# Order of the splits before the fourth step, and of products and adds at both ends of L1 to L3, in a hand-ordered four-layer kernel

## Reference

```python
# L0: gated MLP with a low-rank adapter per block of 32 rows (rank 16, 16 adapters), F = 1376
t = einsum('bri,bni->bnr', A[idx], x);  gate = x @ W_gate.T + 0.5 * B_gate[idx] @ t   # up alike
act = silu(gate) * up
x = x + (act @ W_down.T + 0.5 * B_down[idx] @ (A_down[idx] @ act))
# L1: each block of 32 rows is mixed by the 32 x 32 matrix of its condition
x = x + einsum('bct,bcd->bdt', x, W1[cond])
# L2: base product plus 8 experts of rank 16; the gates are a softmax over the top 2 logits
logits = x @ Wr.T + 5 * one_hot(lang);  topw, topi = top_k(logits, 2)
gates = sum(one_hot(topi) * softmax(topw))
x = x + x @ W2.T + 2.0 * ((x @ A.T) * gates) @ B
# L3: as L1 with other matrices
x = x + einsum('bct,bcd->bdt', x, W3[cond])
```

## Time and profile before

| | before |
|---|---|
| median of 3 runs | 589.03 us (588.71 to 590.17) |
| profiled execution, its own time | 589.99 us |
| its span, first to last instruction | 588.0 us |
| PE busy | 570.5 us |
| DVE busy | 303.8 us |
| ACT busy | 204.5 us |
| POOL busy | 222.1 us |
| granted PE clock, mean | 0.994 |

### The profile page before, as it was taken

The page is one execution under the profiler, slowest core; times in us unless marked ns, Lnnn a source line. Parts: engine busy times, 40 slices in busy tenths (PEclk is TensorE's granted clock), DMA queues, the critical chain, the costliest instruction groups (busy, mean ns, idle before and its releaser), DMA issues.

```text
span 588.0 us, 8799 instructions
## 1 busy us (share of the span) xinstructions
PE 570.5 (97%) x3371; PEld 514.8 (88%) x3371; DVE 303.8 (52%) x697; ACT 204.5 (35%) x413; POOL 222.1 (38%) x227
## 2 busy tenths in 40 slices
PE   5979999999999999999999999999999999999996
PEld 5768998888898989898998989898989898999995
DVE  4885443434344435343434343444444656878776
ACT  4764233233333333332323323232332523333321
POOL 5432133556565656541313131313130212443431
PEclk9979999999999999999999999999999999999999
DMA  8983324253525353543333242424242821233322
GB/s 273 364 284 103 107 79 133 85 173 98 181 92 182 105 175 113 169 135 102 119 93 127 86 134 78 130 82 135 76 136 72 317 62 54 72 137 134 109 89 72
DMA packets 34890, 77.38 MB, mean 132 GB/s; under 512 B 5217, under 2 KB 9633, under 8 KB 34849
## 3 DMA queue, kind: packets, MB, share of 16 engines
q0 software_dynamic: 10752, 37.23, 19.9%
q1 hardware_dynamic: 23952, 39.56, 19.9%
q10 hardware_dynamic: 144, 0.03, 0.0%
HBM read 64.22 MB, written 12.58 MB: 131 GB/s over the span
## 4 chain that ended last, share of the span: by engine, by line
PE 91%; DVE 4%; DMA 2%; issue 1%; ACT 1%; POOL 1%; POOLq 0%; DVEq 0%; ACTq 0%
PE gu_ps L1148 13%; PE gu_ps L1150 13%; PE gu_ps L1149 13%; PE down_ps L1148 8%; PE down_ps L1149 8%; PE down_ps L1150 8%; PE l_ps L1148 5%; PE l_ps L1150 5%; PE l_ps L1149 5%; PE gu_ps L1155 3%; PE gu_ps L1156 3%; PE act_t L1218 3%; PE x2t_ps L1272 1%; DVE w_sb L928 1%; DMA a_raw<-a_all,idx_batch 1%
## 5 line engine op out<-in xcount | busy, mean ns | idle before, releaser
L666 POOL DMA_INDIRECT b_sel_raw<-b_gu,idx_rank x48 | 47.9, 997 | 195.5 <-PE gu_ps L1156 183.2
L1148 PE MATMUL down_ps<-wd_sb,act_hl 128*128 128x288 f32 (+1 forms) x352 | 105.9, 301 | 0.0
L1148 PE MATMUL gu_ps<-w_sb,xt 128*128 128x512 f32 x256 | 104.7, 409 | 0.0
L1149 PE MATMUL down_ps<-wd_sb,act_hl 128*128 128x288 f32 (+1 forms) x352 | 104.6, 297 | 0.0
L1150 PE MATMUL down_ps<-wd_sb,act_hl 128*128 128x288 f32 (+1 forms) x352 | 104.4, 297 | 0.0
L1150 PE MATMUL gu_ps<-w_sb,xt 128*128 128x512 f32 x256 | 100.6, 393 | 0.0
L1149 PE MATMUL gu_ps<-w_sb,xt 128*128 128x512 f32 x256 | 100.2, 391 | 0.0
L666 POOL DMA_INDIRECT a_raw<-a_all,idx_batch x64 | 74.7, 1167 | 57.7 <-DVE wd_sb L928 38.1
L782 ACT CAST act_hl<-act_t 128x256 fp32r<-128x256 f32 (+1 forms) x64 | 27.3, 453 | 136.5 <-PE act_t L1218 136.4
L773 ACT ACTIVATE act<-gu_ps 128x512 f32<-128x512 f32 (+1 forms) x47 | 26.1, 556 | 130.3 <-PE gu_ps L1156 130.3
L928 DVE TENSOR_TENSOR act_hl<-act_t,act_hl 128x256 fp32r<-128x256 f32 (+1 forms) x64 | 32.0, 521 | 75.2 <-ACT act_hl L782 75.1
(11 more groups left out here) (147 smaller groups left out, 1111.9 us busy)
## 6 DMA issues: line engine op xcount, KB each, us to landing
w_sb_raw<-wgu SPq DMA_DIRECT2D x16, 256.0 KB, 9.7
x_res<-x_rows SPq DMA_DIRECT2D x16, 256.0 KB, 2.9
x_after_l<-x_res SPq DMA_DIRECT2D x16, 256.0 KB, 2.3
bd<-bd_hl SPq DMA_DIRECT2D x16, 256.0 KB, 2.0
x<-x_after_l SPq DMA_DIRECT2D x16, 256.0 KB, 2.7
bd_hl<-bd SPq DMA_DIRECT2D x16, 256.0 KB, 4.2
xt_raw<-x_t SPq DMA_DIRECT2D x15, 256.0 KB, 2.5
out<-y SPq DMA_DIRECT2D x15, 256.0 KB, 2.0
```

Of the source, the lines that this page charges most:

```text
L666: nc.gpsimd.indirect_dma_start(out=dst, out_offset=None, in_=table, in_offset=bass.IndirectOffsetOnAxis(ap=idx, axis=0)).then_inc(s, 16)
L1148: pe.matmul(out_, stationary[0], moving[0], start=start, stop=False, skip_group_check=True)
L1149: pe.matmul(out_, stationary[0], moving[1], start=False, stop=False, skip_group_check=True)
```

## The change

Four edits. (1) In the list for step 2 job ("b", 3) stands right behind ("b", 2), and ("act", 0) and ("gate", 2) change places; on PE gate(3) is no longer cut in two by transpose_t(1), which now comes behind transpose_act(0), and gate(4) comes before down(0). (2) At the seam from L0 to L1 to L3, PE does down_adapters(15) before l1(2), and DVE the residual add of tile 15 before add_x2(2). (3) For tiles 1 and 14 DVE does add_x3 before route_weights instead of between route_weights and route_gates. (4) For the last two tiles PE's and DVE's orders are written out. What is computed, and the number of instructions on each engine, stay the same.

```diff
@@ lane_jobs
-                2: [("b", 2), ("adt", 1)] + wd_items(0) + [("act", 0), ("b", 3), ("gate", 2)],
+                2: [("b", 2), ("b", 3), ("adt", 1)] + wd_items(0) + [("gate", 2), ("act", 0)],
@@ block.vector
+                    job_lo(job)
                     if job == ("x1", NT - 1):
                         add_x2(2)
-                    job_lo(job)
...
-            for i in range(NT + 2):
...
+            for i in range(1, NT - 1):
+                low_hgt(i - 1)
+                route_top(i)
+                low_x2t(i + 1)
+                if i == 1 or i == NT - 2:
+                    add_x3(i - 1)
                     route_weights(i)
+                else:
+                    route_weights(i)
                     add_x3(i - 1)
+                route_gates(i)
+                if i + 2 < NT:
                     add_x2(i + 2)
+                if i >= 2:
                     add_y(i - 2)
+            route_top(NT - 1)
+            low_hgt(NT - 2)
+            route_weights(NT - 1)
+            route_gates(NT - 1)
+            add_x3(NT - 2)
+            low_hgt(NT - 1)
+            add_y(NT - 3)
+            add_x3(NT - 1)
+            low_last_x3()
+            add_y(NT - 2)
+            add_y(NT - 1)
@@ block.tensor
             x_a(1)
-            gate(3, 0, HC // 2)
+            whole(gate, 3)
+            transpose_act(0)
             transpose_t(1)
-            gate(3, HC // 2, HC)
-            transpose_act(0)
             whole(up, 3)
             adapters(2)
             adapters(3)
+            whole(gate, 4)
             down(0)
-            whole(gate, 4)
             transpose_act(1)
...
+            down_adapters(NT - 1)
             l1(2)
-            down_adapters(NT - 1)
-            for i in range(1, NT + 2):
...
+            for i in range(1, NT - 2):
+                l2_base(i, 1)
+                transpose_hg(i - 1)
+                l2_base(i, 0, 0, HC // 2)
+                transpose_x2(i + 1)
+                l2_base(i, 0, HC // 2, HC)
+                experts(i - 1)
                 if i >= 2:
                     l3(i - 2)
+                l1(i + 2)
+            l2_base(NT - 2, 1)
+            transpose_hg(NT - 3)
+            transpose_x2(NT - 1)
+            l2_base(NT - 2, 0, 0, HC // 2)
+            experts(NT - 3)
+            l2_base(NT - 2, 0, HC // 2, HC)
+            l3(NT - 4)
+            l2_base(NT - 1, 1)
+            transpose_hg(NT - 2)
+            l2_base(NT - 1, 0)
+            experts(NT - 2)
+            transpose_hg(NT - 1)
+            l3(NT - 3)
+            experts(NT - 1)
+            l3(NT - 2)
+            l3(NT - 1)
```

More of the change, by code:

```diff
@@ L1116, in _ @@
             route_gates(0)
-            for i in range(NT + 2):
[L1119 to L1125, removed]
+            for i in range(1, NT - 1):
[4 more added lines that the diff above has]
+                    add_x3(i - 1)
                     route_weights(i)
[L1127 to L1130, removed]
+                else:
                     route_weights(i)
-                if 1 <= i <= NT:
                     add_x3(i - 1)
[L1134 to L1138, removed]
+                route_gates(i)
+                if i + 2 < NT:
                     add_x2(i + 2)
-                if i >= 2 and i != NT - 1:
+                if i >= 2:
                     add_y(i - 2)
+            route_top(NT - 1)
[9 more added lines that the diff above has]
+            add_y(NT - 1)
         @block.tensor
@@ L1399, in _ @@
             l2_base(0, 0, HC // 2, HC)
+            down_adapters(NT - 1)
             l1(2)
-            down_adapters(NT - 1)
-            for i in range(1, NT + 2):
[L1403 to L1414, removed]
+            for i in range(1, NT - 2):
[5 more added lines that the diff above has]
+                experts(i - 1)
                 if i >= 2:
                     l3(i - 2)
-                if i + 2 < NT:
-                    l1(i + 2)
+                l1(i + 2)
[15 more added lines that the diff above has]
+            l3(NT - 1)
 IDX_BATCH = 1
```

## The result

The changed kernel takes 586.29 us (586.21 to 586.55, 5 runs) against 589.03 us (588.71 to 590.17, 5 runs): a ratio of 0.9947, 95% interval 0.9934 to 0.9959. It is faster by 2.7 us in the medians, 0.47%. The profiled execution's own time is 586.29 us, its span 584.4 us where it was 588.0, the granted clock 1.000 where it was 0.994.

The account below looks back on a forecast made before the run. PE bounds the kernel, busy 570.5 of 588.0 us, leaving idle time and half clock to win. Start -4.57, seam +0.28, end -0.71 sum to -5.0, span 583.0; forecast time 584.4 us, range 582.9 to 586.4.

Parts of the forecast that it names:

- rival C: Start: the wait moves on, down(0) waits 1 to 2 us for chunk 0's activation; 585.9 us, chance 0.11.
- The start: Up to adapters(4): shorter wait before adapters(3) and no half clock, less a new wait at up(3); -4.57 us.
- The seam: L0 to L1: L1036 held by POOL, gain 0.1 at transpose_hg(0); with tile 1 it costs 0.28 us.
- tile 1: After the seam: POOL's low_x3(0) holds L1043 until 495.5, so transpose_hg(1) starts at 496.07 instead of 495.79.
- The end: Last two tiles: add_x3(14) starts earlier, less 0.3 for L1043 held at tile 14; -0.71 us.
- The sum in the span: Whole kernel: start, seam and last two tiles together -5.0 us, span 583.0.
- From the span to the median: Whole kernel: 585.0 for a profiled execution, 584.0 by the median 0.96 below; part may be unwinnable, so 584.4.
- A: Tiles 1 and 14: no hold, L1043 slips past POOL; worth 0.6 + 0.3, 583.5 us, chance 0.15.
- B: Start: the clock falls all the same at waits of 0.9 and 1.1 us; 587.3 us, chance 0.07.
- D: Tiles 2 to 13: the hold spreads, PE waits about 0.6 in each, 7.6 in all; 592.0 us, chance 0.02.
- E: Last two tiles: the end does nothing, its chain as late as before; 585.1 us, chance 0.05.

Follow-up runs that it names:

- e6: The kernel before with 30 transposes of a constant put between adapters(2) and adapters(3), keeping PE busy in its wait: 587.44 us, ratio 0.9969.
- e7: e4 with one wait added, so that POOL begins low_x1(3) only when hg(0) is there: 583.56 us, ratio 0.9897.
- e4: The changed kernel with the old order of add_x3 and route_weights restored at tiles 1 and 14: 584.58 us, ratio 0.9911.
- e2: The changed kernel with the start as before, so only the edits to L1 to L3: 590.04 us, ratio 1.0010.
- e9: The kernel before with one wait added, so that POOL begins low_x1(3) only when hg(0) is there: 589.66 us, ratio 1.0008.
- e5: The changed kernel with two waits added: POOL begins low_x3(0) only after hg(1), low_x3(13) only after hg(14): 583.99 us, ratio 0.9907.

## Why the prediction was right, and where it was not

The time, 586.29, lies in the range, 0.1 us from its upper edge, and the change is faster. It was to be 584.4; the forecast gain was 4.6 us, the measured one 2.7. That it still lies inside is in part luck: the range reached up to 586.4 for rival C, which did not occur. The steps:

- **The start was right almost to the digit.** adapters(3) at 36.78 (36.75 forecast), adapters(4) at 46.50 (46.45), -4.52 us (-4.57); transpose_act(1) at 43.01 (42.96). The new wait inside up(3) is there (0.72, 0.9 forecast), that before adapters(3) is 0.82 (1.1), the one before down(0) is none (0.1). The clock did not fall: 1.00 from 29 to 51 us. e6 shows the split between wait and half clock: 2.0 and 2.5 us, where the text named 2.4 and 2.9 less the new wait, parts that do not add up to its 4.57 exactly.
- **The seam was right:** 0.1 forecast at transpose_hg(0), 0.09 measured, and for the reason given, L1036 held until POOL was through (0.52 us in both kernels). e7 shows the 0.35 behind it.
- **The step that failed is tile 1: "L1043 ... 0.28 inside POOL's 1.30. If it is held as L1036 was, it ends at 495.5."** The mechanism was right, its size was not. I held one instruction under one of POOL's. L1042 was given no hold, and no reason for it, though by the forecast's own times it would have run from 494.18 to 494.46, across POOL's start at 494.22. In fact L1042, a tensor-scalar, was caught first (1.36 us), so that DVE came free only when low_x3(0) ended; and POOL went on at once with low_x1(4), which caught L1043 for another 1.18 us. transpose_hg(1) waited 1.5 us instead of 0.6. The stretch to transpose_hg(2) lost 1.52 us; the forecast, counted from transpose_hg(0), had a loss of 0.38 (0.28 and the 0.1 gained at the seam). POOL's second instruction stands in the trace of before: behind the low parts of x3(0) to x3(11) the next x1's follows without a gap. The rows that I took from there show only the first.
- **The end: -0.71 forecast, -0.50 measured.** L1042 of tile 14 was caught (1.42 us) where I had L1043; the waits of transpose_hg(14) and (15) were 0.11 and 0.43. The last chain, add_x3(14) to l3(14), was 579.12 - 576.24 = 2.88 as forecast. With tile 14 in the old order, and so without the hold, the end gives 0.94 (e4).
- **The sum in the span** was to be -5.0 and is -3.6: 1.1 of the missing 1.4 us is tile 1, 0.2 the end.
- **From the span to the median** another 0.9 is lost, -3.6 to -2.7, and here the doubt in the text was the right one. The before that was profiled was one of the slower executions, 0.96 us above the median; the changed kernel's profiled execution is its own median. I had taken 0.4 of these 0.96 us as lost; it was all of them. The clocks of the five runs of before in that set are not on record, but those of 42 later ones are. In the first 15 they form two groups: 0.996 to 0.997 with 588.92 to 589.29 us, and 0.990 to 0.994 with 589.98 to 590.50. In the other 27 the groups overlap (0.993 goes with 588.62 to 590.19), and three had 1.000 and took 587.52, 587.52 and 587.65. The profiles agree: from adapters(3) to adapters(4) it is 12.30 us in before, 11.21 in e2 and 11.20 in e9, with the same order of instructions, and 9.67 in e6 at full clock. So the half clock costs that kernel a different length in each execution, and an execution that had little of it had less to win back. The changed kernel's runs lie within 0.34 us. Against the median of those 42 runs, 589.30, it gains 3.0 us.
- **Rivals.** A (no hold) fell at the profile, and e5 shows what the absence of a hold is worth: 1.9 us of span against the changed kernel, not 0.9. Its time of 583.5 was near (e5 took 583.99). B, C, D and E did not occur: no fall of the clock, no wait at down(0), 68.38 us between transpose_hg(2) and transpose_hg(13) as before, and 0.50 us won at the end. (D's 7.6 us should be 7.2, 12 times 0.6.) What the prediction lacked was a rival with a longer hold.

## What to carry to other kernels

When an instruction of VectorE with its operands in SBUF is moved, look not only at what it waits for but at what GpSimd does at that moment and right after: here GpSimd's low parts of 1.3 us each made one instruction of 0.29 us 1.36 us long and the next, of 0.17 us, 1.18. In tiles 2 to 13 of the old order L1043 ends only 0.13 to 0.19 us before GpSimd's low part begins, so a small move is enough. Where two limits lie on one place, as at the seam, taking away one gives little (0.09 us, or nothing) and both together 0.44. And where a kernel's runs fall into groups, take the profiled execution's group into account before its time is set against a median.

## What the runs showed of the hardware

- The hold of VectorE by GpSimd reached a tensor-scalar too, not only instructions with two tensors from SBUF. L1042, a tensor-scalar of a 128x8 constant with two per-partition scalars from SBUF, was held for 1.36, 1.35 and 1.42 us in three places (0.29 otherwise), each time until within 0.03 us of the end of a GpSimd tensor-tensor. The profile puts its start 0.04, 0.04 and 0.09 us ahead of GpSimd's, so the starts do not tell which engine came first. Beside GpSimd and still at their usual length ran a tensor-scalar on one column with two immediates (L1034, 0.15 us inside low_x1(3)), a reciprocal on one column (L1035, 0.16 there), and in L1 to L3 the instructions with an operand in PSUM (the add of y, L1078, 0.68 us in 14 tiles beside GpSimd and 0.69 in the one apart). The Trainium skill (SBUF — State Buffer, "Who interferes with whom") has the hold for an instruction with two SBUF inputs beside a GpSimd instruction that reads SBUF; L1043 and L1036 bear it out with 1.18 and 0.52 us. The same section says that a tensor-scalar, too, can contend with GpSimd, in a two-port mode that it enters when its operands meet certain conditions. L1042 fits that; whether this mode or its two scalars from SBUF brought on the hold, no run here tells apart.
- An idle stretch of 3.5 us on PE cost another 2.5 us behind its end in the profiled execution, by half clock (1.2 GHz, 0.50), and how much differed from one execution to the next of the same kernel (granted clock 0.990 to 1.000, 587.52 to 590.97 us). With PE kept busy in it (e6) the clock stayed at 2.4 GHz. Waits of 0.72 and 0.82 us with 3.1 us of work between them were followed by no fall in the changed kernel (granted clock 1.000 in all five runs).
- Short waits are no guarantee: behind 0.68 and 0.77 us, with 1.0 us of work between them, the clock fell to 0.50 in e6's profiled execution and stood at 1.00 in that of before.
